# Perceiver block tail on one Trainium2 core: v projected ahead of k, q turned between the two products with Wo, token shift as two scaled matrix products

## Chip, cores and metric

One core of a Trainium2 chip. The metric is the device time in microseconds (us) of one execution of the whole program; lower is better.

## The reference, cut to what matters

The input is x (128 tokens, 256 channels) and a context of 12,544 rows of 256 channels. The block has three residual parts, each on a layer norm of x.

```python
x = x + xattn(layernorm(x), ctx)      # similarity over 12,544 context rows, softmax, mixing, W_qv
x = x + attn(layernorm(x))            # 16 heads, no softmax:
    # q, k, v = x@Wq+bq, x@Wk+bk, x@Wv+bv;  q, k = rope(q), rope(k)
    # score = q k^T / sqrt(16);  ctx = score v;  ctx @ Wo + bo
x = x + ffn(layernorm(x))
    # x_prev = concat([zeros, x[:, :-1]], axis=1)
    # xr = mu_r * x + (1 - mu_r) * x_prev;  xk = mu_k * x + (1 - mu_k) * x_prev
    # sigmoid(xr @ W_r) * (relu(xk @ W_k)**2 @ W_v)
```

As there is no softmax in the second part, the kernel computes k^T v first (16x16 blocks on the diagonal of a 256x256 matrix, kept by a mask) and multiplies it with Wo and then with q.

## The kernel before, in words

All order is written out by hand: each engine has one instruction stream (`block.sync`, `gpsimd`, `scalar`, `vector`, `tensor`), and the streams meet in semaphores alone. Nothing overtakes on an engine, so an instruction that waits holds all behind it.

**The sweep, 0 to 93 us.** The context comes in 25 chunks of 512 rows (the last has 256), first as keys (transposed), then as rows, through a ring of ten buffers in SBUF; SP issues all these loads. For most key chunks ScalarE makes a high part in a reduced 32-bit format (L476), VectorE subtracts it to get the low part (L681), and TensorE makes the scores in three products (L908, L912, L915); every fourth chunk is taken in plain fp32 (L898). VectorE keeps the running maximum (L703). In the second half, for each rows chunk k:

- TensorE turns the probabilities of chunk k+2 in four passes (L929), then runs `mix(k)` (L958, L960), which needs the low part of the rows and the low part of the turned probabilities.
- ScalarE exponentiates (L495), copies the turned probabilities as their high part (L508), and casts the first half of rows chunk k+2 (L476).
- POOL casts the second half of rows chunk k (L429, loop L425). This needs a free buffer pair, so `mix(k-4)` must be done. Between casts POOL has small jobs on weights and biases, at k = 15 to 19: among them `mean_const` (L445) and `mu_left`, that is 1 - mu for r and k (L447), at k = 17, and at k = 18 `w_neg_mean` (L452) and the sum of two weight blocks of 128x512 (L456), which the tail needs.
- VectorE, in this order: low part of the turned probabilities of k (`probs_low`, L710), then low part of rows chunk k+2 (`rows_low`, L681), which needs both casts of that chunk.

**The tail, 93 to 113 us.** TensorE: x1 is summed (L977), then `project` (L1051) for k, v and q, with the variance of x1 (L1061) between the first and the second half of the first projection; v^T times the rotated bias of k (L1074) and v^T times rotated k (L1078); `open_sums` (L972) and the part of x1 that is kept (L1082); masked product times Wo (L1086), in two halves; q turned (L1089), in two halves; product with q (L1094); means (L1103); two idle passes; the transposed and normed x2 (L1110), made by a product with a diagonal matrix; two more idle passes (`keep_warm`, L883, whose results nobody reads); k's projection (L1116), r's (L1122) and the last product (L1128). VectorE: variance, then for k `rope` (L819, L822), v scaled (L835), `rope_sum` (L828), `rope` for q, the mask (L841), `rope_sum` for q, bias of q added to the turned q (L847), statistics of x2 (L673 to L677), diagonal matrix (L853), shift (L859), square of relu (L864), gate (L870), sum (L875). POOL raises the variance to the power -1/2 (L421). ScalarE copies the two Wo results (L645) and x2 (L648), scales the transposed x2 by mu for k (L651) and for r (L659), relu (L665), sigmoid (L667).

In the shift before, the transposed x2 is in PSUM. ScalarE writes mu * x for all tokens, then VectorE adds (1 - mu) times the columns 0 to 126 to the columns 1 to 127: once for each half and each of k and r.

An fp32 product appears as two records on TensorE, a transpose as one.

Of the kernel before, what the change touches and what calls it, by code (L numbers as in the profile page):

```python
# [7 lines left out]
P = 128  # L8
# [3 lines left out]
ALU = mybir.AluOpType  # L12
ACT = mybir.ActivationFunctionType
# [4 lines left out]
DH = D // P  # L18
# [22 lines left out]
WB_Q = 4 * DH  # L41
WB_K = WB_Q + DH
WB_V = WB_K + DH
# [7 lines left out]
VC_W1, VC_W2, VC_W3, VC_MUR, VC_MUK, VC_BQ, VC_BQ_SWAPPED = (DH * n for n in range(7))  # L51
# [6 lines left out]
def build(nc, x, keys_in, keys_last_in, rows_in, rows_last_in, weights_in, vec_in, bias_in, const_in, out):  # L58
# [37 lines left out]
    with ExitStack() as stack:  # L96
        def sb(name, shape, dt=F32):
            return stack.enter_context(nc.sbuf_tensor(name, shape, dt))
# [4 lines left out]
        def sem(name):  # L103
            return stack.enter_context(nc.semaphore(name))
# [9 lines left out]
        ident = sb("ident", [P, P])  # L114
        ones = sb("ones", [P, P])
        idle = sb("idle", [P, CHUNK], BF16)
        w = sb("w", [P, WB, D])
        vec = sb("vec", [P, VC])
# [22 lines left out]
        ln_rstd = sb("ln_rstd", [P, 3])  # L141
# [27 lines left out]
        mean_const = sb("mean_const", [P, 1])  # L169
        mu_left = sb("mu_left", [P, 2 * DH])  # L170
        d_inv = sb("d_inv", [P, 1])
# [12 lines left out]
        with_cos, with_sin, rotated = scratch[:, 5:7, :], scratch[:, 7:9, :], scratch[:, 9:11, :]  # L184
        v = scratch[:, 11, :]
# [6 lines left out]
        rstd_diagonal = sb("rstd_diagonal", [P, P])  # L192

        xk_t = sb("xk_t", [P, DH, P])
        xr_t = sb("xr_t", [P, DH, P])
# [9 lines left out]
        banks = [scores_ps[:, g, h * CHUNK:(h + 1) * CHUNK] for g in range(3) for h in range(2)]  # L205
# [19 lines left out]
        tail_idle_ps = banks[2]  # L225
        x2n_ps = (banks[0][:, 0:P], banks[5][:, 0:P])
        k_t_ps = (banks[1][:, 0:P], banks[2][:, 0:P])
# [61 lines left out]
        mean_const_done = sem("mean_const_done")  # L289
        mu_left_done = sem("mu_left_done")  # L290
        x_c_done = sem("x_c_done")
# [47 lines left out]
        x2_done = sem("x2_done")  # L339
        diagonal_done = sem("diagonal_done")  # L340
        x2n_turned = sem("x2n_turned")

        xk_scaled = sem("xk_scaled")
        xr_scaled = sem("xr_scaled")
        xk_done = sem("xk_done")
# [64 lines left out]
        def _(pool):  # L410
# [8 lines left out]
            def power(n):  # L419
                pool.wait_ge(var_done, n + 1)  # L420
                nc.gpsimd.tensor_tensor(out=ln_rstd[:, n:n + 1], in0=ln_var[:, n:n + 1], in1=minus_half[:, :],  # L421
                                        op=ALU.pow).then_inc(rstd_done, 1)

            power(0)
            for k in range(EARLY, FULL):  # L425
                item, use = CHUNKS + k, row_use(k)
# [16 lines left out]
                if k == 17:  # L443
                    pool.wait_ge(b_mean_summed, 1)
                    nc.gpsimd.tensor_tensor(out=mean_const[:, :], in0=b_mean_sum[:, :], in1=ln_mv[:, 0, 0:1], op=ALU.add)\  # L445
                        .then_inc(mean_const_done, 1)
                    nc.gpsimd.tensor_scalar(mu_left[:, :], vec[:, VC_MUR:VC_MUR + 2 * DH], -1.0, 1.0,  # L447
                                            ALU.mult, ALU.add).then_inc(mu_left_done, 1)
                if k == 18:
# [16 lines left out]
        def _(act):  # L466
# [182 lines left out]
            for a in range(DH):  # L649
                act.wait_ge(x2n_turned, a + 1)  # L650
                nc.scalar.activation(xk_t[:, a, :], x2n_ps[a], ACT.Copy, scale=vec[:, VC_MUK + a:VC_MUK + a + 1])\  # L651
                    .then_inc(xk_scaled, 1)
            act.wait_ge(mean_const_done, 1)
            act.wait_ge(x2_mean_summed, 1)
            nc.scalar.activation(x2_mean[:, :], x2_mean_ps, ACT.Identity, bias=mean_const[:, :], scale=-1.0)\
                .then_inc(x2_mean_done, 1)
            for a in range(DH):
                act.wait_ge(xk_done, a + 1)
                nc.scalar.activation(xr_t[:, a, :], x2n_ps[a], ACT.Copy, scale=vec[:, VC_MUR + a:VC_MUR + a + 1])\  # L659
                    .then_inc(xr_scaled, 1)  # L660
            act.wait_ge(x2_mean_done, 1)
# [8 lines left out]
        def _(dve):  # L670
# [159 lines left out]

            dve.wait_ge(rstd_done, 2)
            dve.wait_ge(k_rows_projected, 1)
            rope(0, k_ps)
            dve.wait_ge(v_projected, 1)
            nc.vector.scalar_tensor_tensor(v, v_ps, ln_rstd[:, 1:2], bv_rows, ALU.mult, ALU.add).then_inc(v_done, 1)  # L835
            rope_sum(0)
# [8 lines left out]
            for a in range(DH):  # L845
# [6 lines left out]
            dve.wait_ge(rstd_done, 3)  # L852
            nc.vector.tensor_scalar(rstd_diagonal[:, :], ident[:, :], ln_rstd[:, 2:3], None, ALU.mult)\  # L853
                .then_inc(diagonal_done, 1)
            dve.wait_ge(mu_left_done, 1)
            for mixed_t, left, scaled, done in ((xk_t, DH, xk_scaled, xk_done), (xr_t, 0, xr_scaled, xr_done)):
                for a in range(DH):
                    dve.wait_ge(scaled, a + 1)
                    nc.vector.scalar_tensor_tensor(mixed_t[:, a, 1:P], x2n_ps[a][:, 0:P - 1],  # L859
                                                   mu_left[:, left + a:left + a + 1], mixed_t[:, a, 1:P],  # L860
                                                   ALU.mult, ALU.add).then_inc(done, 1)
# [17 lines left out]
        def _(pe):  # L879
# [208 lines left out]
            for a in range(DH):  # L1088
# [18 lines left out]
            pe.wait_ge(x2_c_done, 1)  # L1107
            pe.wait_ge(diagonal_done, 1)
# [80 lines left out]
```

## Time and profile before

| | us |
|---|---|
| median of 3 runs | 114.57 |
| lowest, highest | 114.46, 115.26 |
| the profiled execution | 115.56 |
| its span, first to last instruction | 113.8 |
| TensorE busy in it | 106.9 |
| VectorE busy | 92.9 |
| ScalarE busy | 80.4 |
| POOL busy | 29.0 |

The granted TensorE clock was 1.00 over the whole span, the higher of its two levels (2.4 GHz). Lines of the timeline give start, duration, engine, line of the kernel, operation, destination and sources, shapes, count, and in brackets the idle time before with what ended it. VectorE, ScalarE and TensorE start an instruction somewhat before the record of the last one ends, so records overlap.

### The profile page before, as it was taken

How to read it: one execution, taken by the hardware profiler on the slowest of the kernel's cores; microseconds unless marked ns; L12 is line 12 of the kernel's file. 1: busy time of each engine (PE TensorE's matmuls, PEld its weight loads, DVE VectorE, ACT ScalarE, POOL GpSimd, SP SyncE). 2: the span in 40 equal slices, each digit the busy share in tenths (PEclk: the TensorE clock that was granted, in tenths of full speed). 3: DMA queues.
4: the chain of work that ended last, by engine and by line, in shares of the span. 5: the costliest groups of instructions: out<-in, count | busy, mean ns of one | idle time of the engine just before them, and what ended most of it. 6: DMA issues, size and time to landing. Idle time of an engine off the chain costs nothing.

```text
span 113.8 us, 1825 instructions
## 1 busy us (share of the span) xinstructions
PE 106.9 (94%) x578; PEld 85.0 (75%) x579; DVE 92.9 (82%) x149; ACT 80.4 (71%) x168; POOL 29.0 (25%) x42
## 2 busy tenths in 40 slices
PE   5978999999999999999999999999899999898890
PEld 2426858585758588889999898999787899787680
DVE  1538999998999999988997999895999955693342
ACT  5039493889999874999999998999968444303450
POOL 2100000000000016204767567799621000100100
PEclk9999999999999999999999999999999999999999
DMA  3999999999999999999999999940000000000001
GB/s 94 353 370 418 415 419 422 419 422 416 419 425 418 419 408 415 422 354 383 351 396 414 416 423 421 419 169 0 6 0 0 0 6 0 0 0 0 6 3 46
DMA packets 8220, 29.82 MB, mean 262 GB/s; under 512 B 1042, under 2 KB 1298, under 8 KB 8082
## 3 DMA queue, kind: packets, MB, share of 16 engines
q1 hardware_dynamic: 8064, 29.69, 65.5%
q8 instruction: 5, 0.08, 0.3%
q14 instruction: 5, 0.04, 0.1%
q10 hardware_dynamic: 146, 0.01, 0.1%
HBM read 29.57 MB, written 0.13 MB: 261 GB/s over the span
## 4 chain that ended last, share of the span: by engine, by line
PE 85%; DMA 5%; DVE 3%; ACT 2%; issue 1%; SPq 1%; POOL 1%; DVEq 0%; ACTq 0%; POOLq 0%
PE mixed_ps L958 17%; PE scores_ps L929 9%; PE mixed_ps L960 8%; PE scores_ps L898 8%; PE scores_ps L908 8%; PE scores_ps L915 8%; PE scores_ps L912 7%; DMA raw<-keys_dram 5%; PE scores_ps L940 3%; PE scores_ps L1051 2%; PE mixed_ps L1103 1%; PE side_ps L977 1%; PE scores_ps L1116 1%; PE side_ps L1094 1%; PE scores_ps L977 1%
## 5 line engine op out<-in xcount | busy, mean ns | idle before, releaser
L681 DVE TENSOR_TENSOR pair<-raw,pair 128x1024 fp32r<-128x1024 f32 (+1 forms) x41 | 50.1, 1234 | 5.0 <-ACT pair L476 3.7
L476 ACT ACTIVATE pair<-raw 128x512 fp32r<-128x512 f32 (+1 forms) x41 | 33.4, 814 | 9.1 <-DMA raw<-keys_dram 5.7
L429 POOL CAST pair<-raw 128x512 fp32r<-128x512 f32 x22 | 21.3, 969 | 54.8 <-DMA raw<-rows_dram 39.3
L958 PE MATMUL mixed_ps<-pair,turned_high 128*128 128x512 f32 x84 | 32.2, 417 | 0.5 <-DVE turned_low L710 0.4
L960 PE MATMUL mixed_ps<-pair,turned_low 128*128 128x256 f32 x84 | 23.6, 281 | 0.0
L958 PEld LDWEIGHTS mixed_ps<-pair,turned_high 128*128 128x128 f32 x84 | 15.8, 188 | 4.2 <-issue 1.3
L703 DVE TENSOR_SCALAR_CACHE_REDUCE neg_scores<-scores_ps,neg_max 128x1024 f32<-128x1024 f32 (+2 forms) x14 | 16.1, 1147 | 0.4
L960 PEld LDWEIGHTS mixed_ps<-pair,turned_low 128*128 128x128 f32 x84 | 15.9, 190 | 0.0
L710 DVE TENSOR_TENSOR turned_low<-scores_ps,turned_high 128x512 fp32r<-128x512 f32 (+1 forms) x23 | 15.4, 671 | 0.3 <-ACT turned_high L508 0.3
L929 PE MATMUL scores_ps<-ident,neg_scores 128*128 128x128 f32 x98 | 14.6, 272 | 0.0
L908 PE MATMUL scores_ps<-pair,q_high 128*128 128x512 f32 x36 | 13.4, 453 | 1.1 <-ACT pair L476 1.1
L508 ACT ACTIVATE turned_high<-scores_ps 128x512 fp32r<-128x512 f32 (+1 forms) x23 | 13.2, 574 | 1.2 <-PE scores_ps L929 1.2
L495 ACT ACTIVATE neg_scores<-neg_scores,neg_max 128x1024 f32<-128x1024 f32 (+2 forms) x14 | 13.6, 974 | 0.1
L929 PEld LDWEIGHTS scores_ps<-ident,neg_scores 128*128 128x128 f32 x98 | 11.7, 140 | 1.6 <-ACT neg_scores L495 0.3
L898 PE MATMUL scores_ps<-raw,q_t 128*128 128x512 f32 (+1 forms) x28 | 12.4, 564 | 0.0
L915 PE MATMUL scores_ps<-pair,q_high 128*128 128x512 f32 x36 | 11.3, 396 | 0.0
L912 PE MATMUL scores_ps<-pair,q_low 128*128 128x512 f32 x36 | 11.2, 392 | 0.0
L908 PEld LDWEIGHTS scores_ps<-pair,q_high 128*128 128x128 f32 x36 | 6.6, 188 | 5.3 <-issue 4.3
L915 PEld LDWEIGHTS scores_ps<-pair,q_high 128*128 128x128 f32 x36 | 6.6, 188 | 2.0 <-DVE pair L681 0.6
L912 PEld LDWEIGHTS scores_ps<-pair,q_low 128*128 128x128 f32 x36 | 6.8, 188 | 1.5
L898 PEld LDWEIGHTS scores_ps<-raw,q_t 128*128 128x128 f32 x28 | 5.1, 189 | 3.4 <-issue 2.9
L421 POOL TENSOR_TENSOR ln_rstd<-ln_var,minus_half 128x1 f32<-128x1 f32 x3 | 1.7, 557 | 21.6 <-DVE ln_var L815 12.6
(187 smaller groups left out, 121.8 us busy)
## 6 DMA issues: line engine op xcount, KB each, us to landing
raw<-keys_dram SPq DMA_DIRECT2D x24, 512.0 KB, 10.1
raw<-rows_dram SPq DMA_DIRECT2D x24, 512.0 KB, 7.8
w<-weights_dram SPq DMA_DIRECT2D x1, 1792.0 KB, 9.6
w<-weights_dram SPq DMA_DIRECT2D x2, 512.0 KB, 11.6
const<-const_dram SPq DMA_DIRECT2D x1, 832.0 KB, 11.2
raw<-keys_last_dram SPq DMA_DIRECT2D x1, 256.0 KB, 8.4
raw<-rows_last_dram SPq DMA_DIRECT2D x1, 256.0 KB, 6.5
x_sb<-x_dram SPq DMA_DIRECT2D x1, 128.0 KB, 2.2
```

What stands on the lines that cost most here:

```text
L429: nc.gpsimd.tensor_copy(out=pair[:, use % PAIR_BUFS, 0, 2 * D:4 * D], in_=raw[:, slot(item), 2 * D:4 * D])\
L476: nc.scalar.activation(pair[:, use % PAIR_BUFS, 0, 0:columns], raw[:, slot(item), 0:columns], ACT.Copy)\
L681: nc.vector.tensor_tensor(out=pair[:, use % PAIR_BUFS, 1, 0:columns], in0=raw[:, slot(item), 0:columns], in1=pair[:, use % PAIR_BUFS, 0, 0 ...
L703: nc.vector.tensor_scalar(neg_scores[:, first_col:last_col], scores_ps[:, first // 2 % 3, scores_at:scores_at + last_col - first_col], -1. ...
L710: nc.vector.tensor_tensor(out=turned_low[:, k % TURNED_BUFS, 0:width_of(k)], in0=probs_turned_ps[k % TURNED_BUFS][:, 0:width_of(k)], in1=t ...
L898: last = nc.tensor.matmul(out_ps, q_t[:, a, :], keys_part(raw[:, slot(k), :], k, a), start=(a == 0), stop=(a == DH - 1))
L908: nc.tensor.matmul(out_ps, q_high[:, a, :], keys_part(high, k, a), start=(a == 0), stop=False)
L912: nc.tensor.matmul(out_ps, q_low[:, a, :], keys_part(high, k, a), start=False, stop=False)
L915: last = nc.tensor.matmul(out_ps, q_high[:, a, :], keys_part(low, k, a), start=False, stop=(a == DH - 1))
L929: last = nc.tensor.transpose(probs_turned_ps[k % TURNED_BUFS][:, t * P:(t + 1) * P], neg_scores[:, col:col + P], ident[:, :])
L958: nc.tensor.matmul(mixed_ps[:, :].rearrange("p (h d) -> p h d", h=2), probs_high, both[:, :, t * D:(t + 1) * D], start=(k == EARLY and t = ...
L960: last = nc.tensor.matmul(mixed_ps[:, 0:D], probs_low, rows_tile(high, t), start=False, stop=(k == LATE - 1 and end))
```

## The change

Constants: two 128x128 matrices are made on POOL right after the first power. `next_token` has ones on the diagonal beside the main one (it moves each token to the next), `same_less_next` is the identity less `next_token`. `mu_left` goes.

```diff
             power(0)
+            nc.gpsimd.memset(next_token[:, :], 0.0).then_inc(next_zeroed, 1)
+            pool.wait_ge(next_zeroed, 1)
+            nc.gpsimd.affine_select(out=next_token[:, :], in_=next_token[:, :], compare_op=ALU.not_equal, fill=1.0,
+                                    base=1, pattern=[[-1, P]], channel_multiplier=1).then_inc(shifts_set, 1)
+            pool.wait_ge(shifts_set, 1)
+            nc.gpsimd.tensor_tensor(out=same_less_next[:, :], in0=ident[:, :], in1=next_token[:, :], op=ALU.subtract)\
+                .then_inc(shifts_set, 1)
...
-                    nc.gpsimd.tensor_scalar(mu_left[:, :], vec[:, VC_MUR:VC_MUR + 2 * DH], -1.0, 1.0,
-                                            ALU.mult, ALU.add).then_inc(mu_left_done, 1)
```

v ahead of k, on VectorE and on TensorE:

```diff
             dve.wait_ge(rstd_done, 2)
+            dve.wait_ge(v_projected, 1)
+            nc.vector.scalar_tensor_tensor(v, v_ps, ln_rstd[:, 1:2], bv_rows, ALU.mult, ALU.add).then_inc(v_done, 1)
             dve.wait_ge(k_rows_projected, 1)
             rope(0, k_ps)
-            dve.wait_ge(v_projected, 1)
-            nc.vector.scalar_tensor_tensor(v, v_ps, ln_rstd[:, 1:2], bv_rows, ALU.mult, ALU.add).then_inc(v_done, 1)
             rope_sum(0)
...
-            project(k_ps, WB_K, 0)
+            project(v_ps, WB_V, 0)
...
-            project(k_ps, WB_K, 1).then_inc(k_rows_projected, 1)
-            for out_ps, block_row, done in ((v_ps, WB_V, v_projected), (q_ps, WB_Q, q_projected)):
+            project(v_ps, WB_V, 1).then_inc(v_projected, 1)
+            for out_ps, block_row, done in ((k_ps, WB_K, k_rows_projected), (q_ps, WB_Q, q_projected)):
```

q turned between the two halves of the product with Wo:

```diff
                 nc.tensor.matmul(attn_ps[a], vk[:, a, :], wo_c[:, a, :], start=True, stop=True).then_inc(attn_summed, 1)
-            pe.wait_ge(rotated_done, 2)
-            for a in range(DH):
-                nc.tensor.transpose(q_turn_ps[a], rotated[:, 1, a * P:(a + 1) * P], ident[:, :])\
-                    .then_inc(q_rot_turned, 1)
+                if a == 0:
+                    pe.wait_ge(rotated_done, 2)
+                    for b in range(DH):
+                        nc.tensor.transpose(q_turn_ps[b], rotated[:, 1, b * P:(b + 1) * P], ident[:, :])\
+                            .then_inc(q_rot_turned, 1)
```

The shift: TensorE makes the previous token (`prev_ps`) and the step from it to the token itself (`step_ps`) with the two constants scaled by the reciprocal deviation; ScalarE copies the first, VectorE makes mu * step + prev for all 128 tokens in place of 127.

```diff
+                act.wait_ge(prev_turned, a + 1)
+                nc.scalar.activation(prev_t[:, a, :], prev_ps[a], ACT.Copy).then_inc(prev_copied, 1)
-                nc.scalar.activation(xk_t[:, a, :], x2n_ps[a], ACT.Copy, scale=vec[:, VC_MUK + a:VC_MUK + a + 1])\
-                    .then_inc(xk_scaled, 1)
...
-                nc.scalar.activation(xr_t[:, a, :], x2n_ps[a], ACT.Copy, scale=vec[:, VC_MUR + a:VC_MUR + a + 1])\
-                    .then_inc(xr_scaled, 1)
...
-            nc.vector.tensor_scalar(rstd_diagonal[:, :], ident[:, :], ln_rstd[:, 2:3], None, ALU.mult)\
-                .then_inc(diagonal_done, 1)
+            nc.vector.tensor_scalar(to_next[:, :], next_token[:, :], ln_rstd[:, 2:3], None, ALU.mult)\
+                .then_inc(to_next_done, 1)
+            nc.vector.tensor_scalar(to_step[:, :], same_less_next[:, :], ln_rstd[:, 2:3], None, ALU.mult)\
+                .then_inc(to_step_done, 1)
...
-                    nc.vector.scalar_tensor_tensor(mixed_t[:, a, 1:P], x2n_ps[a][:, 0:P - 1],
-                                                   mu_left[:, left + a:left + a + 1], mixed_t[:, a, 1:P],
+                    dve.wait_ge(prev_copied, a + 1)
+                    dve.wait_ge(x2n_turned, a + 1)
+                    nc.vector.scalar_tensor_tensor(mixed_t[:, a, :], step_ps[a], vec[:, col + a:col + a + 1], prev_t[:, a, :],
                                                    ALU.mult, ALU.add).then_inc(done, 1)
...
-                nc.tensor.matmul(x2n_ps[a], x2_c[:, a * P:(a + 1) * P], rstd_diagonal[:, :], start=True, stop=True)\
+                nc.tensor.matmul(prev_ps[a], x2_c[:, a * P:(a + 1) * P], to_next[:, :], start=True, stop=True)\
+                    .then_inc(prev_turned, 1)
+            pe.wait_ge(to_step_done, 1)
+            for a in range(DH):
+                nc.tensor.matmul(step_ps[a], x2_c[:, a * P:(a + 1) * P], to_step[:, :], start=True, stop=True)\
                     .then_inc(x2n_turned, 1)
             keep_warm(WARM_SHIFT, tail_idle_ps)
```

## Rows read from the trace of the kernel before

**Rows 1.** The page, part 4: shares of the chain that ended last, by engine.

```profile
PE 85%; DMA 5%; DVE 3%; ACT 2%; issue 1%; SPq 1%; POOL 1%; DVEq 0%; ACTq 0%; POOLq 0%
```

**Rows 2.** The chain in order of time, 78 to 82 us: start, duration, what.

```profile
78.69 0.62 POOL pair L429
...
79.33 0.92 DVE pair L681
...
80.47 0.70 DVE turned_low L710
...
81.30 0.47 PE mixed_ps L958
```

**Rows 3.** Timeline of the second half of the sweep, 73 to 84 us.

```profile
74.47 1.22 DVE L681 TENSOR_TENSOR pair<-raw,pair 128x1024 fp32r<-128x1024 f32 x1
74.54 1.20 POOL L447 TENSOR_SCALAR mu_left<-vec 128x4 f32<-128x4 f32 x1
...
75.63 0.62 ACT L476 ACTIVATE pair<-raw 128x512 fp32r<-128x512 f32 x1
...
75.68 0.61 POOL L429 CAST pair<-raw 128x512 fp32r<-128x512 f32 x1
...
76.36 1.23 DVE L681 TENSOR_TENSOR pair<-raw,pair 128x1024 fp32r<-128x1024 f32 x1
76.41 2.33 POOL L456 TENSOR_TENSOR w<-w 128x512 f32<-128x512 f32 x1
...
76.97 0.48 PE L958 MATMUL mixed_ps<-pair,turned_high 128*128 128x512 f32 x1
...
78.82 0.48 PE L958 MATMUL mixed_ps<-pair,turned_high 128*128 128x512 f32 x1
...
79.39 1.63 POOL L429 CAST pair<-raw 128x512 fp32r<-128x512 f32 x1
...
83.07 0.61 POOL L429 CAST pair<-raw 128x512 fp32r<-128x512 f32 x1 [1.49 <-PE mixed_ps L960]
83.18 1.58 DVE L681 TENSOR_TENSOR pair<-raw,pair 128x1024 fp32r<-128x1024 f32 x1
```

**Rows 4.** Timeline of the attention part of the tail, 97 to 105 us.

```profile
97.95 1.54 PE L1051 MATMUL scores_ps<-w,x_t 128*128 128x256 f32 x6
98.96 0.48 DVE L819 SCALAR_TENSOR_TENSOR neg_scores<-scores_ps,ln_rstd,const 128x256 f32<-128x256 f32 x1 [0.68 <-POOL ln_rstd L421]
...
100.15 0.42 DVE L828 TENSOR_TENSOR neg_scores<-neg_scores 128x256 f32<-128x256 f32 x1
...
101.71 0.41 DVE L828 TENSOR_TENSOR neg_scores<-neg_scores 128x256 f32<-128x256 f32 x1
...
101.86 1.03 PE L1086 MATMUL scores_ps<-wo_c,neg_scores 128*128 128x257 f32 x4
102.49 0.82 ACT L645 ACTIVATE attn<-scores_ps 128x257 f32<-128x257 f32 x2 [4.79 <-PE scores_ps L1086]
...
102.73 0.38 PE L1089 MATMUL scores_ps<-ident,neg_scores 128*128 128x128 f32 x2
...
103.45 1.13 PE L1094 MATMUL side_ps<-attn,neg_scores 128*128 128x256 f32 x4 [0.34 <-DVE neg_scores L847]
```

**Rows 5.** Timeline of the token shift, 106 to 109 us.

```profile
106.56 0.68 PE L1110 MATMUL scores_ps<-rstd_diagonal,x_c 128*128 128x128 f32 x4
...
107.05 0.63 ACT L651 ACTIVATE xk_t<-scores_ps,vec 128x128 f32<-128x128 f32 x2 [1.58 <-PE scores_ps L1110]
107.08 0.59 PE L883 MATMUL scores_ps<-idle 128*128 128x512 bf16 x2
107.52 0.61 DVE L859 SCALAR_TENSOR_TENSOR xk_t<-scores_ps,mu_left,xk_t 128x127 f32<-128x127 f32 x2 [1.11 <-ACT xk_t L651]
...
107.92 1.16 PE L1116 MATMUL scores_ps<-xk_t,w 128*128 128x128 f32 x8 [0.25 <-DVE xk_t L859]
```

**Rows 6.** Waits of TensorE in the whole span: who for whom, us, times, longest.

```profile
PE scores_ps L908 <- ACT pair L476: 1.1, 1, 1.1
```

More of the change, by code:

```diff
@@ L114, in build @@
         ident = sb("ident", [P, P])
+        next_token = sb("next_token", [P, P])
+        same_less_next = sb("same_less_next", [P, P])
         ones = sb("ones", [P, P])
@@ L169, in build @@
         mean_const = sb("mean_const", [P, 1])
-        mu_left = sb("mu_left", [P, 2 * DH])
         d_inv = sb("d_inv", [P, 1])
@@ L191, in build @@
         x2 = sb("x2", [P, D])
-        rstd_diagonal = sb("rstd_diagonal", [P, P])
+        to_next = sb("to_next", [P, P])
+        to_step = sb("to_step", [P, P])
+        prev_t = sb("prev_t", [P, DH, P])
         xk_t = sb("xk_t", [P, DH, P])
@@ L225, in build @@
         tail_idle_ps = banks[2]
-        x2n_ps = (banks[0][:, 0:P], banks[5][:, 0:P])
+        prev_ps = (banks[0][:, 0:P], banks[5][:, 0:P])
+        step_ps = (banks[3][:, 0:P], banks[4][:, 0:P])
         k_t_ps = (banks[1][:, 0:P], banks[2][:, 0:P])
@@ L289, in build @@
         mean_const_done = sem("mean_const_done")
-        mu_left_done = sem("mu_left_done")
         x_c_done = sem("x_c_done")
@@ L339, in build @@
         x2_done = sem("x2_done")
-        diagonal_done = sem("diagonal_done")
+        next_zeroed = sem("next_zeroed")
+        shifts_set = sem("shifts_set")
+        prev_turned = sem("prev_turned")
+        prev_copied = sem("prev_copied")
+        to_next_done = sem("to_next_done")
+        to_step_done = sem("to_step_done")
         x2n_turned = sem("x2n_turned")
-        xk_scaled = sem("xk_scaled")
-        xr_scaled = sem("xr_scaled")
         xk_done = sem("xk_done")
@@ L649, in _ @@
             for a in range(DH):
-                act.wait_ge(x2n_turned, a + 1)
-                nc.scalar.activation(xk_t[:, a, :], x2n_ps[a], ACT.Copy, scale=vec[:, VC_MUK + a:VC_MUK + a + 1])\
-                    .then_inc(xk_scaled, 1)
+                act.wait_ge(prev_turned, a + 1)
+                nc.scalar.activation(prev_t[:, a, :], prev_ps[a], ACT.Copy).then_inc(prev_copied, 1)
             act.wait_ge(mean_const_done, 1)
@@ L656, in _ @@
                 .then_inc(x2_mean_done, 1)
-            for a in range(DH):
-                act.wait_ge(xk_done, a + 1)
-                nc.scalar.activation(xr_t[:, a, :], x2n_ps[a], ACT.Copy, scale=vec[:, VC_MUR + a:VC_MUR + a + 1])\
-                    .then_inc(xr_scaled, 1)
             act.wait_ge(x2_mean_done, 1)
@@ L852, in _ @@
             dve.wait_ge(rstd_done, 3)
-            nc.vector.tensor_scalar(rstd_diagonal[:, :], ident[:, :], ln_rstd[:, 2:3], None, ALU.mult)\
-                .then_inc(diagonal_done, 1)
-            dve.wait_ge(mu_left_done, 1)
-            for mixed_t, left, scaled, done in ((xk_t, DH, xk_scaled, xk_done), (xr_t, 0, xr_scaled, xr_done)):
+            dve.wait_ge(shifts_set, 2)
+            nc.vector.tensor_scalar(to_next[:, :], next_token[:, :], ln_rstd[:, 2:3], None, ALU.mult)\
+                .then_inc(to_next_done, 1)
+            nc.vector.tensor_scalar(to_step[:, :], same_less_next[:, :], ln_rstd[:, 2:3], None, ALU.mult)\
+                .then_inc(to_step_done, 1)
+            for mixed_t, col, done in ((xk_t, VC_MUK, xk_done), (xr_t, VC_MUR, xr_done)):
                 for a in range(DH):
-                    dve.wait_ge(scaled, a + 1)
-                    nc.vector.scalar_tensor_tensor(mixed_t[:, a, 1:P], x2n_ps[a][:, 0:P - 1],
-                                                   mu_left[:, left + a:left + a + 1], mixed_t[:, a, 1:P],
+                    dve.wait_ge(prev_copied, a + 1)
+                    dve.wait_ge(x2n_turned, a + 1)
+                    nc.vector.scalar_tensor_tensor(mixed_t[:, a, :], step_ps[a], vec[:, col + a:col + a + 1], prev_t[:, a, :],
                                                    ALU.mult, ALU.add).then_inc(done, 1)
@@ L1086, in _ @@
                 nc.tensor.matmul(attn_ps[a], vk[:, a, :], wo_c[:, a, :], start=True, stop=True).then_inc(attn_summed, 1)
-            pe.wait_ge(rotated_done, 2)
-            for a in range(DH):
-                nc.tensor.transpose(q_turn_ps[a], rotated[:, 1, a * P:(a + 1) * P], ident[:, :])\
-                    .then_inc(q_rot_turned, 1)
+                if a == 0:
[3 more added lines that the diff above has]
+                            .then_inc(q_rot_turned, 1)
             for a in range(DH):
@@ L1107, in _ @@
             pe.wait_ge(x2_c_done, 1)
-            pe.wait_ge(diagonal_done, 1)
+            pe.wait_ge(to_next_done, 1)
             for a in range(DH):
-                nc.tensor.matmul(x2n_ps[a], x2_c[:, a * P:(a + 1) * P], rstd_diagonal[:, :], start=True, stop=True)\
+                nc.tensor.matmul(prev_ps[a], x2_c[:, a * P:(a + 1) * P], to_next[:, :], start=True, stop=True)\
[3 more added lines that the diff above has]
+                nc.tensor.matmul(step_ps[a], x2_c[:, a * P:(a + 1) * P], to_step[:, :], start=True, stop=True)\
                     .then_inc(x2n_turned, 1)
```

## The prediction, made before the change was run

> **What bounds the kernel now.** I read first the shares of the chain that ended last, then that chain in order of time, then the timeline of each stretch that the diff touches. The shares say that TensorE is on the path for 85% of the span [rows 1]: work on another engine pays only where TensorE waits for it. The chain in order leaves TensorE in two places that the edits reach. The first is the middle of the key sweep: at 78.69 the path goes to POOL's cast of rows chunk 19, from there to VectorE's subtraction for the same chunk at 79.33, to its subtraction for the turned probabilities at 80.47, and back to TensorE at 81.30 [rows 2]. The second is the tail from 97 us on, a string of short steps, where I followed which operand of each product comes last. The profiled execution took 115.56 us with a span of 113.8; the median shown is 114.57. I work with differences in the span and put them on the median.
>
> **Part 1, v ahead of k.** The same projections run in the same slots, only the contents change places. The six passes from 97.95 end at 99.49, the end of the second matrix, now k's [rows 4]. VectorE starts at 98.96, when the reciprocal deviation is there, and its three products before the sum at 100.15 are spaced (100.15 - 98.96)/3 = 0.40. Now v's comes at 98.96 and k's could start at 99.36, but k lands at 99.49 and is seen some 0.04 later: 99.53, a loss of 0.17. The sum of the rotation now stands right behind the second product it reads, with nothing between: 99.53 + 0.40 + 0.48 (that product's own time) + 0.04 = 100.45 against 100.15, 0.30 late, and done at 100.87. Behind it in VectorE's queue stand q's two rotations, the two masks, and q's sum: that one moves from 101.71 to 102.01 and ends at 102.42.
> On TensorE v is ready earlier, so the first two v products start without their wait; before, that wait was at most some 0.2 us. The products with k's rotation then wait for 100.87 + 0.05, and the first pass after a wait costs 0.10 more (four passes of 0.215 with a last one of 0.38 would make 1.03, the row at 103.45 has 1.13). So they begin in effect at 101.02. Before they began 1.0 us (four passes of 0.11, the opening 0.11, four passes of 0.11) ahead of the product with Wo at 101.86, at 100.86. So the first product with Wo moves from 101.86 to 102.02: this part costs 0.16.
>
> **Part 2, q turned between the two products with Wo.** Before: four passes of (102.73 - 101.86)/4 = 0.22, two turns of 0.11, then VectorE adds the bias and the product with q starts at 103.45; its second half is long fed. ScalarE's copies of the two Wo results take 0.82 together, 0.39 each. After: Wo's first half 102.02 to 102.46, then the turns, for which q's sum must be there: 102.42 + 0.05 = 102.47, on the edge, and with the refill of 0.10 they start at 102.57; second half of Wo 102.79 to its result at 103.39; copy 103.42 to 103.81. TensorE sees a ScalarE result later than one of VectorE (I take 0.12; 0.05 and 0.2 are the ends), so the last two passes start at 103.96 in place of 103.88 (103.45 + 2 x 0.215). The end of x2's sum is 0.06 late by this (104.64 for 104.58). With part 2 alone the same sum gives 0.2 early, with every handover of part 1 at 0.1 more it gives 0.35 late. So parts 1 and 2 cancel: +0.06, ends -0.25 and +0.35. What is late next is no longer q's turn but ScalarE's second copy.
>
> **Part 3, the token shift.** VectorE scales two 128x128 matrices, not one: the first is on the path as before, the second is done 0.2 to 0.3 us later, while TensorE runs the first four passes. Before: products from 106.56, ScalarE's scaling from 107.05, VectorE's sum from 107.52, k's projection from 107.92 [rows 5]. After: four passes for the previous token, four more for the step (0.44), results at about 107.52 + 0.06 (the step) and 107.49 (ScalarE's copy, 0.3, and its handover). The sum starts at 107.56 and k's projection could at 107.95. But the two idle passes meant to keep the clock up, 0.22 each [rows 5], now stand behind eight passes, not four, and end at 106.56 + 0.06 + 0.07 + 0.88 + 0.43 = 108.00. The projection starts there, without a refill, where it started in effect at 107.92 + 0.10. Gain 0.02; ends -0.1 and +0.15. That r's input comes 0.3 us sooner and that ScalarE loses two operations is worth nothing: TensorE runs k's, r's and the last projection back to back from 107.92 on. Three small POOL operations at the start run before any rows come; beside them q is made, and TensorE later waits 1.1 us for ScalarE's first split of keys anyway [rows 6], so they are hidden up to 1.1 us.
>
> **Part 4, what leaves POOL.** With the shift on TensorE the four-column operation mu_left (1.20 us at 74.54) is gone from POOL's queue. This is the largest effect I find, through who gets the SBUF port. The rows show exclusion. When VectorE's subtraction with two SBUF inputs starts first, POOL stands: started 0.05 or 0.06 later, a cast of 0.61 takes 1.63, the sum of two weight blocks (w, 128x512) 2.33, the tiny mu_left 1.20. When a cast starts first, by 0.11 (83.07 against 83.18), VectorE's 1.23 becomes 1.58, ending 1.08 after the cast [rows 3]. The Trainium skill, SBUF — State Buffer, "Who interferes with whom", says the same of such pairs: whichever issues first has the shared port for its whole instruction. By that rule POOL's head start below decides, and the time would be the forecast's.
> Now chunk 18. Its cast needs product 14, which began two cadences of 78.82 - 76.97 = 1.85 before product 16 (76.97), so was over by 75.1. It then stands behind VectorE's subtraction of 74.47 and ends 1.69 after that start (79.33 to 79.39 + 1.63 likewise): 76.16 for 76.29. The weight sum, 0.12 behind, starts at 76.28 and not 76.41. VectorE's subtraction at 76.36 is held by ScalarE's cast (75.63 + 0.62 = 76.25, plus 0.11), so stays. The order turns: POOL is first by 0.08.
> The weight sum then takes its own 2.33 - 1.08 + 0.05 = 1.30 and ends at 77.58; VectorE's subtraction ends 1.08 later, 78.65 for 77.59; product 17 starts at 79.39 for 78.82, 0.57 late. But the cast of 19, at 78.69 before, no longer queues behind a blocked weight sum. If VectorE gets the port at the seam, that cast ends at 79.11, the subtraction of 19 starts at 79.17, product 18 at 81.25, and from there VectorE starts each subtraction before POOL's cast of the chunk. Before it lost that race three times (81.07, 83.18, 85.28; one row stands), with 1.50 + 0.60 = 2.10 per chunk against TensorE's cadence of 1.85. Products 19, 20 and 21 then keep 1.85: 0.8 us gained. If POOL's next cast takes the port once more, product 17 slips to 79.97, and the same steps leave 0.25. The rows at 75.68 to 76.41 show VectorE slipping in between two POOL operations, which leans to 0.8; no row has it already waiting there. I take 0.5.
>
> **Sum.** +0.06 - 0.02 - 0.5 = about -0.5: 114.57 - 0.5 = 114.1 us.
>
> **The rivals.** A, the forecast, 114.1 us, 45%; its own range is 113.7 to 114.4.
> B, no change: 0.08 us is less than the smallest lead with which POOL wins in the rows (0.11), and VectorE wins at -0.05, so the weight sum may still come second. Then it ends where it did, 76.36 + 2.38 = 78.74, cast 19 follows at 78.69, and only the tail is left: 114.57 + 0.04 = 114.6 us, 30%. For it: the lead hangs on a ScalarE cast. Against it: 0.08 lies nearer to 0.11 than to -0.05.
> C, slower: k's rotation behind v. The 0.30 goes down VectorE's queue to q's sum, and the turns that need it now stand before Wo's second half. It decides once that sum is later than 102.46, when TensorE has done Wo's first half; by my sum it is at 102.47. From there each 0.1 us goes through Wo, the copy and the last product. With B and the upper end of +0.35: 114.9 us, 12%. For it: no slack at all. Against it: it wants each handover above its row.
> D, both gains whole: the port at 0.8 and the tail at its lower end of -0.25: 113.5 us, 13%. Against it: k's delay of 0.17 follows from the order of the passes alone.
>
> **How the numbers follow.** A, B and D and most of C lie between 113.4 and 114.9, the range. About 1%, 1.15 us, is what a measurement of this kernel can tell from no change. Only the far side of D passes it downwards: 0.09. Upwards it wants C and something unseen beside: 0.03. Within 1%: 0.88.
>
> **What would show it.** Part 1: k's first product on VectorE near 99.5, its sum near 100.45 (relative to the variance), q's sum after 102. Part 2: the last product's second half released by ScalarE's second copy. Part 3: idle passes ending at the start of k's projection; r never waiting. Part 4: POOL's weight sum 1.3 us long and VectorE's subtraction beside it 2.3, and no subtraction of 1.58 afterwards. Wrong would be: a weight sum still 2.33 long with a large gain, k's rotation not late, or x2's sum earlier by more than 0.25.

## The result, and the profile after the change

The change takes 114.03 us (median of 20 runs, 113.5 to 115.38) against 114.94 us before (20 runs, 114.34 to 116.41): ratio 0.9914, 95% interval 0.9887 to 0.9941. The ratio leaves out the few executions that were over 1.5% slower than the fastest of the same kernel; it stands for 0.99 us (0.68 to 1.30), where the medians of all runs differ by 0.91. The forecast was a gain of 0.5 us, from 114.57 to 114.1, with a range that holds 114.03. The time came out as forecast, the gain twice as large: the kernel before, 114.57 in the 3 runs that the forecast started from, takes 114.94 in 20. The profiled execution of the change took 113.73 us with a span of 111.9.

First the chain of the page, part 4, of the changed kernel: shares by engine.

```profile
PE 64%; DMA 17%; DVE 10%; issue 3%; ACT 2%; POOL 1%; SPq 1%; DVEq 0%; ACTq 0%; POOLq 0%
```

Against [rows 1] this looks like another kernel, but most of it is the start of the span: in this execution the chain happens to lead back to the loading of keys. The two spans differ by 1.9 us, and half of that is there before the sweep reaches the place that the diff touches: VectorE's subtraction for chunk 17, which stood at 74.47 in [rows 3], stands at 73.53 here. Over all profiles of this study that moment lies between 73.2 and 74.7 us with no relation to the edits (73.34 and 74.65 in two kernels that keep the start of before, e12 and e11 below), so I count from it. From there to the variance of x1 it was 98.12 - 74.47 = 23.65 us and is 96.18 - 73.53 = 22.65: the 1.00 us of the change. Here is the place (product k is `mix(k)`, the products of TensorE for rows chunk k), in the timeline of the changed kernel (L687 is the old L681, L716 the old L710, L442 the cast, L467 the sum of the two weight blocks):

```profile
73.53 1.22 DVE L687 TENSOR_TENSOR pair<-raw,pair 128x1024 fp32r<-128x1024 f32 x1
74.12 1.10 POOL L442 CAST pair<-raw 128x512 fp32r<-128x512 f32 x1 [0.48 <-PE mixed_ps L968]
...
75.33 1.28 POOL L467 TENSOR_TENSOR w<-w 128x512 f32<-128x512 f32 x1
75.42 2.28 DVE L687 TENSOR_TENSOR pair<-raw,pair 128x1024 fp32r<-128x1024 f32 x1
76.57 1.60 POOL L442 CAST pair<-raw 128x512 fp32r<-128x512 f32 x1
77.62 0.68 DVE L716 TENSOR_TENSOR turned_low<-scores_ps,turned_high 128x512 fp32r<-128x512 f32 x1
...
78.22 1.21 DVE L687 TENSOR_TENSOR pair<-raw,pair 128x1024 fp32r<-128x1024 f32 x1
78.27 1.64 POOL L442 CAST pair<-raw 128x512 fp32r<-128x512 f32 x1
78.45 0.47 PE L966 MATMUL mixed_ps<-pair,turned_high 128*128 128x512 f32 x1 [0.32 <-DVE turned_low L716]
```

Read it against [rows 3]. There the weight sum began 0.05 us behind the subtraction and took 2.33 us; here it begins 0.09 us ahead and takes 1.28, and the subtraction takes 2.28. Product 17 (78.45) is late by half a microsecond, 2.42 us after product 16 (76.03) where the cadence is 1.85, and no later subtraction is stretched. Products 18 to 21 follow at the cadence, and 22 in 1.63 us:

```profile
76.03 0.48 PE L966 MATMUL mixed_ps<-pair,turned_high 128*128 128x512 f32 x1
...
80.29 0.48 PE L966 MATMUL mixed_ps<-pair,turned_high 128*128 128x512 f32 x1
...
82.14 0.48 PE L966 MATMUL mixed_ps<-pair,turned_high 128*128 128x512 f32 x1
...
87.48 0.48 PE L966 MATMUL mixed_ps<-pair,turned_high 128*128 128x512 f32 x1
```

Product 22 begins 11.45 us after product 16, before it was 12.39. The tail, in the timeline of the changed kernel, gives nothing and takes a little:

```profile
96.18 0.16 DVE L821 TENSOR_SCALAR ln_var<-scores_ps 128x1 f32<-128x1 f32 x1 [0.19 <-PE scores_ps L1069]
97.02 0.48 DVE L839 SCALAR_TENSOR_TENSOR neg_scores<-scores_ps,ln_rstd,const 128x256 f32<-128x256 f32 x1 [0.68 <-POOL ln_rstd L427]
97.58 0.48 DVE L825 SCALAR_TENSOR_TENSOR neg_scores<-scores_ps,ln_rstd,const 128x256 f32<-128x256 f32 x1
...
98.56 0.43 DVE L834 TENSOR_TENSOR neg_scores<-neg_scores 128x256 f32<-128x256 f32 x1
99.05 0.71 PE L1086 MATMUL scores_ps<-neg_scores 128*128 128x128 f32 x4 [0.19 <-DVE neg_scores L834]
...
100.56 0.22 PEld L1098 LDWEIGHTS scores_ps<-ident,neg_scores 128*128 128x128 f32 x2 [0.17 <-DVE neg_scores L834]
100.63 0.38 PE L1098 MATMUL scores_ps<-ident,neg_scores 128*128 128x128 f32 x2
...
101.48 0.39 ACT L656 ACTIVATE attn<-scores_ps 128x257 f32<-128x257 f32 x1 [0.27 <-PE scores_ps L1094]
102.72 0.43 DVE L679 BATCH_NORM_STATS2 ln_six<-side_ps 128x6 f32<-128x256 f32 x1 [1.22 <-PE side_ps L1103]
...
105.67 0.82 DVE L868 SCALAR_TENSOR_TENSOR xk_t<-scores_ps,vec,prev_t 128x128 f32<-128x128 f32 x2 [0.96 <-ACT prev_t L662]
...
106.07 0.99 PEld L1129 LDWEIGHTS scores_ps<-xk_t,w 128*128 128x128 f32 x8 [0.35 <-DVE xk_t L868]
...
109.30 0.48 DVE L883 TENSOR_TENSOR x<-mixed_out,x 128x128 f32<-128x128 f32 x2
```

From the variance of x1 to the statistics of x2 it is 102.72 - 96.18 = 6.54 us (before 6.50), from there to the last sums 109.30 - 102.72 = 6.58 (before 6.51). k's rotation starts where its projection lands (97.58), its sum comes 2.38 us after the variance (before 2.03), and ScalarE's second copy (101.48) is what the last product waits for. PEld is TensorE's loading of weights: for the turns of q (100.56) and for k's projection (106.07) it sat idle until VectorE's result was there. The three stretches add up to 1.00 - 0.04 - 0.07 = 0.89 us.

### The profile page after: what moved, and what is told of

The parts are those of the page before. It is cut to its first block, busy times and chain, and to the rows that moved or that the text cites. A ratio compares the mean times of both kernels' runs of the same rounds, so it can differ in the third digit from the quotient of the medians.

```text
span 111.9 us, 1840 instructions
## 1 busy us (share of the span) xinstructions
PE 106.8 (95%) x583; PEld 85.3 (76%) x583; DVE 93.5 (84%) x150; ACT 79.6 (71%) x166; POOL 31.8 (28%) x44
## 4 chain that ended last, share of the span: by engine, by line
PE 64%; DMA 17%; DVE 10%; issue 3%; ACT 2%; POOL 1%; SPq 1%; DVEq 0%; ACTq 0%; POOLq 0%
DMA raw<-keys_dram 17%; PE mixed_ps L966 15%; PE scores_ps L937 8%; PE mixed_ps L968 8%; DVE pair L687 6%; PE scores_ps L906 4%; PE scores_ps L923 4%; PE scores_ps L948 3%; PE scores_ps L920 3%; PE scores_ps L916 3%; ACT pair L487 2%; PE scores_ps L1059 2%; PE mixed_ps L1112 1%; PE side_ps L985 1%; DVE turned_low L716 1%
## 5 line engine op out<-in xcount | busy, mean ns | idle before, releaser
L687 DVE TENSOR_TENSOR pair<-raw,pair 128x1024 fp32r<-128x1024 f32 (+1 forms) x41 | 50.4, 1243 | 2.5 <-ACT pair L487 2.4
L442 POOL CAST pair<-raw 128x512 fp32r<-128x512 f32 x22 | 25.3, 1151 | 51.0 <-DMA raw<-rows_dram 38.4
L716 DVE TENSOR_TENSOR turned_low<-scores_ps,turned_high 128x512 fp32r<-128x512 f32 (+1 forms) x23 | 15.4, 671 | 0.4 <-ACT turned_high L519 0.3
```

Source lines behind the costliest of these rows:

```text
L442: nc.gpsimd.tensor_copy(out=pair[:, use % PAIR_BUFS, 0, 2 * D:4 * D], in_=raw[:, slot(item), 2 * D:4 * D])\
L687: nc.vector.tensor_tensor(out=pair[:, use % PAIR_BUFS, 1, 0:columns], in0=raw[:, slot(item), 0:columns], in1=pair[:, use % PAIR_BUFS, 0, 0 ...
L716: nc.vector.tensor_tensor(out=turned_low[:, k % TURNED_BUFS, 0:width_of(k)], in0=probs_turned_ps[k % TURNED_BUFS][:, 0:width_of(k)], in1=t ...
```

## The experiments

The theory: the change gains because mu_left leaves POOL's queue. That moves the weight sum from just behind to just ahead of VectorE's subtraction, so it gets first the way into SBUF that the two engines share (the port); afterwards VectorE wins each race against a cast and TensorE keeps its cadence. The rivals: the gain is in the tail, or POOL's queue was only too long. Each run is read in three stretches: A from the subtraction of chunk 17 to the variance of x1, B from there to the statistics of x2, C from there to the last sums.

**e1, mu_left early.** On the kernel before:

```diff
             power(0)
+            pool.wait_ge(vec_loaded, 16)
+            nc.gpsimd.tensor_scalar(mu_left[:, :], vec[:, VC_MUR:VC_MUR + 2 * DH], -1.0, 1.0,
+                                    ALU.mult, ALU.add).then_inc(mu_left_done, 1)
...
-                    nc.gpsimd.tensor_scalar(mu_left[:, :], vec[:, VC_MUR:VC_MUR + 2 * DH], -1.0, 1.0,
-                                            ALU.mult, ALU.add).then_inc(mu_left_done, 1)
```

> The kernel before, with one move: POOL makes mu_left right after its first power, at about 5 us, and no longer between the casts at 74.5 us. The tail stays as before. Port theory: the sum of the two weight blocks starts just ahead of VectorE's subtraction, is 1.3 us long and not 2.33, the subtraction beside it 2.3, no later subtraction is 1.58 long, and the whole gain of the change is here: ratio to before 0.991 to 0.992 (0.9 to 1.0 us). Rival, the tail's edits bring the gain: ratio 1.000.

Measured: 114.31 us against 114.82, ratio 0.9942 (0.9912 to 0.9972). The timeline of e1 has the pattern of the change:

```profile
75.23 1.29 POOL L457 TENSOR_TENSOR w<-w 128x512 f32<-128x512 f32 x1
75.32 2.28 DVE L682 TENSOR_TENSOR pair<-raw,pair 128x1024 fp32r<-128x1024 f32 x1
```

A is 22.62 us, 1.03 less than before, with the tail of before. The sweep's gain is thus all in this one move. The ratio missed the expected 0.991 to 0.992, and the profile shows a part of the reason: C took 7.58 us in place of 6.51. The windows of e1 show the cause (the column before the last two is the granted clock):

```profile
103.00:104.00 1.00, 1.00 (x11) 1.00 (x11) 0.34 (x2) 0.38 (x1) 0.54 (x1) 1.00 0.00 0
104.00:105.00 1.00, 0.92 (x5) 0.70 (x6) 0.29 (x1) 0.00 (x0) 0.01 (x1) 0.69 0.00 0
105.00:106.00 1.00, 1.00 (x6) 0.55 (x4) 0.25 (x1) 0.66 (x3) 0.00 (x0) 0.50 0.07 16
106.00:107.00 1.00, 1.00 (x6) 0.85 (x5) 0.91 (x4) 1.00 (x5) 0.00 (x0) 0.50 0.03 8
107.00:108.00 1.00, 1.00 (x7) 1.00 (x7) 0.24 (x1) 0.42 (x2) 0.00 (x0) 0.60 0.00 0
```

TensorE's clock went from 2.4 to 1.2 GHz for some 3 us. Four of the 12 runs of e1 have a mean clock of 0.985 like this one, and 2 of the 31 runs of before beside it. Without these runs the medians are 114.09 and 114.81, a difference of 0.72 us, still short of the 1.03 of stretch A; the rest is not explained. That was a second question: does the change also keep the clock up, and by which part?

**e2, mu_left kept.** The changed kernel with the operation put back at k = 17, its result unused.

```diff
                     nc.gpsimd.tensor_tensor(out=mean_const[:, :], in0=b_mean_sum[:, :], in1=ln_mv[:, 0, 0:1], op=ALU.add)\
                         .then_inc(mean_const_done, 1)
+                    nc.gpsimd.tensor_scalar(mu_left[:, :], vec[:, VC_MUR:VC_MUR + 2 * DH], -1.0, 1.0,
+                                            ALU.mult, ALU.add).then_inc(mu_left_done, 1)
```

> The changed kernel, with the four-column mu_left kept in its old place in POOL's queue (nobody reads it). Port theory: the weight sum starts behind VectorE's subtraction again and takes 2.33 us, three subtractions take 1.58, and the gain is gone: ratio to before 1.000 to 1.001. Rival, the tail brings the gain: ratio 0.991 as for the change.

Measured: 114.87 us, ratio 1.0008 (0.9979 to 1.0037). A is 23.65 as before. The whole tail of the change is in this kernel, and it shows no gain in the median.

**e3, the weight sum 0.15 us later.**

```diff
                     pool.wait_ge(w3_scaled, DH)
+                    nc.gpsimd.tensor_tensor(out=spare[:, :], in0=b_mean[:, 0:1], in1=b_mean[:, 1:2], op=ALU.add)
                     nc.gpsimd.tensor_tensor(out=w[:, 0:DH, :], in0=w[:, 0:DH, :], in1=w[:, 3 * DH:4 * DH, :],
```

> The changed kernel with one one-column addition (0.15 us from start to start, result unused) put right ahead of the weight sum in POOL's queue. Port theory: POOL's lead of 0.09 us turns into a lag of 0.06, so VectorE gets the port, the weight sum takes 2.3 us, and some 0.9 us are lost for 0.15 us of work: ratio to before 1.000. Rival, POOL's queue was only too long by 1.2 us: 0.15 us at most are lost, ratio 0.991 to 0.993.

Measured: 115.05 us, ratio 0.9995 (0.9963 to 1.0028). The timeline of e3:

```profile
76.27 0.19 POOL L468 TENSOR_TENSOR spare<-b_mean 128x1 f32<-128x1 f32 x1
76.36 1.23 DVE L689 TENSOR_TENSOR pair<-raw,pair 128x1024 fp32r<-128x1024 f32 x1
76.42 2.32 POOL L469 TENSOR_TENSOR w<-w 128x512 f32<-128x512 f32 x1
...
81.07 1.58 DVE L689 TENSOR_TENSOR pair<-raw,pair 128x1024 fp32r<-128x1024 f32 x1
...
83.18 1.59 DVE L689 TENSOR_TENSOR pair<-raw,pair 128x1024 fp32r<-128x1024 f32 x1
```

The lead of 0.09 us has become a lag of 0.06, and A is 23.66: one column of work on POOL, 0.15 us, costs 1.0 us. That rules out the length of the queue and leaves the order of two starts.

**e4, k ahead of v again**, q still turned between the products with Wo.

```diff
-            project(v_ps, WB_V, 0)
+            project(k_ps, WB_K, 0)
...
-            for out_ps, block_row, done in ((k_ps, WB_K, k_rows_projected), (q_ps, WB_Q, q_projected)):
+            for out_ps, block_row, done in ((v_ps, WB_V, v_projected), (q_ps, WB_Q, q_projected)):
```

VectorE's order goes back with it: k's rotation, then v.

> The changed kernel with k projected and rotated ahead of v again, q still turned between the two products with Wo. By my sum v first costs 0.16 us on the way to the product with Wo and takes away the 0.2 us that the earlier turn would give: x2's sum ends 0.2 to 0.3 us sooner, measured from the variance of x1, ratio to before 0.989 (the change 0.991). Rival, v first is neutral or a gain: x2's sum ends no sooner.

Measured: 113.87 us, ratio 0.9892 (0.9857 to 0.9928); B is 102.72 - 96.46 = 6.26 us, 0.28 less than in the change. Here v first is a loss.

**e5, the weight sum last.**

```diff
-                if k == 18:
-                    pool.wait_ge(w3_scaled, DH)
-                    nc.gpsimd.tensor_tensor(out=w[:, 0:DH, :], in0=w[:, 0:DH, :], in1=w[:, 3 * DH:4 * DH, :],
-                                            op=ALU.add).then_inc(w_combined, 1)
...
+            pool.wait_ge(w3_scaled, DH)
+            pool.wait_ge(total_inv_done, 1)
+            nc.gpsimd.tensor_tensor(out=w[:, 0:DH, :], in0=w[:, 0:DH, :], in1=w[:, 3 * DH:4 * DH, :],
+                                    op=ALU.add).then_inc(w_combined, 1)
             power(1)
```

> The changed kernel with the sum of the two weight blocks moved behind POOL's last cast, where it also waits for VectorE's reciprocal of the total, so that it runs beside instructions with one SBUF input. Port theory: the sum is 1.3 us long, no VectorE subtraction is longer than 1.25 us, product 17 is no longer 0.5 us late, and that time is gained on top of the change: ratio to before 0.986 to 0.987. Rival, what matters is only the three stretched subtractions that the change already removed: ratio 0.991 as for the change.

Measured: 113.16 us, ratio 0.9846 (0.9806 to 0.9886); A is 95.52 - 73.43 = 22.09, another 0.56 us less, which is product 17's delay. The timeline of e5, POOL alone from 86 us on:

```profile
87.30 1.29 POOL L471 TENSOR_TENSOR w<-w 128x512 f32<-128x512 f32 x1 [2.88 <-DVE total_inv L772]
```

The windows of TensorE, VectorE and the rest from 75 to 90 us, of e5 (the first number after the stretch's length is TensorE busy):

```profile
75.00:90.00 15.00, 15.00 (x102) 13.63 (x101) 13.71 (x20) 12.85 (x27) 7.64 (x9) 1.00 0.01 2
```

and of the kernel before:

```profile
75.00:90.00 15.00, 14.54 (x89) 12.29 (x88) 13.82 (x17) 12.12 (x28) 7.80 (x10) 1.00 0.02 8
```

TensorE has no gap left there, and POOL is busy for about as long. The counts of products, 102 and 89, are not of the same work: at 90 us e5 is some 2.5 us further on than before. Nor is the gap of 0.46 us the whole loss of before, since the records run on into the waits: before, four turns start at 82.77 and last 0.60 us in the record, and the product behind them starts 0.63 us after them, where at 78.47 it follows in 0.35. The loss is read from A.

**e6, e4 and e5 together.**

> e5 with k projected and rotated ahead of v as in e4. If the two gains lie in different stretches they add: 0.5 us in the sweep and 0.28 us between the variance of x1 and the statistics of x2, ratio to before 0.983 to 0.985. Rival, one of them hides the other: ratio 0.986 to 0.988.

Measured: 113.14 us, ratio 0.9833 (0.9796 to 0.987). A is 22.09 and B 6.25: both gains stand side by side. The intervals of e5 and e6 overlap, so that e6 is the faster of the two rests on B alone. Both beat the kernel before, and by A also the change.

**e7, the old shift** (with mu_left at the start) under the new order of v, k and q: the diff of the shift undone.

> The changed kernel with the token shift of before (mu_left made at the start, as in e1), v first and q turned between kept. Statistics of x2 to the last sum: 6.5 us as before, 0.07 less than in the change. The granted clock fell to half for 3 us of the shift stage in 4 of 12 runs of e1 and in 2 of 31 of before, and in none of the 52 runs with the new shift. Theory that the new shift prevents it: some runs here have a mean clock of 0.985 and are 1.1 us longer, ratio to before 0.991 to 0.995. Rival, that the new order of v, k and q prevents it: no such run, ratio 0.990 to 0.991.

Measured: 113.87 us, ratio 0.9899 (0.986 to 0.9939); C is 6.50, and none of 6 runs has the low clock. The new shift costs 0.08 us.

**e8, the shift alone**: the changed kernel with k first and q turned behind both products.

> The changed kernel with k ahead of v and q turned behind both products with Wo, so that the constants, the new shift and POOL's shorter queue are all that is left of the change. Variance of x1 to statistics of x2: 6.50 as before (6.54 in the change), then 6.58 as in the change: ratio to before 0.991. If the new shift prevents the fall of the clock, no run has 0.985; if the order of v, k and q does, about a third of the runs have it and the ratio is 0.993 or more.

Measured: 114.01 us, ratio 0.9913 (0.9873 to 0.9952); B is 6.50. One of 8 runs has the low clock, the profiled one, with C = 8.01 us. So the new shift does not prevent the fall. TensorE waits once in the attention part of this kernel, ahead of the product with q; its weight loads sit idle there for 0.6 us. In the change they sit idle twice, 0.31 and 0.33 us, ahead of either half of that product. Waits of TensorE in e8, 100 to 104 us:

```profile
PE side_ps L1102 <- DVE neg_scores L853: 0.3, 1, 0.3
```

**e9, no idle passes**: e6 without the call below.

```diff
-            keep_warm(WARM_SHIFT, tail_idle_ps)
```

> e6 without the two idle passes between the shift's products and k's projection. In the change the projection starts where these passes end, though its input is there some 0.1 us earlier. If they are only in the way: statistics of x2 to the last sum 6.48 to 6.52 us in place of 6.59, and the clock stays. If they are needed: the clock falls in some runs, which are 1.1 us or more longer.

Measured: 113.35 us, ratio 0.9846 (0.9797 to 0.9896); C is 6.58, not the expected 6.48 to 6.52. TensorE now waits for VectorE where the passes stood:

```profile
106.23 1.19 PE L1128 MATMUL scores_ps<-xk_t,w 128*128 128x128 f32 x8 [0.29 <-DVE xk_t L868]
```

So the idle passes did not set the start of k's projection; its input did. None of 6 runs has the low clock.

**e10, v first alone**: the changed kernel with q turned behind both products.

> The changed kernel with q turned behind both products with Wo again, v still first. By my sum v first alone costs 0.16 us: variance of x1 to statistics of x2 6.66 us (before 6.50, the change 6.54), ratio to before 0.991 to 0.993. Theory that the turn between the products keeps the clock up: some runs here have a mean clock of 0.985. Rival, v first does it: none.

Measured: 115.1 us, ratio 0.9982 (0.994 to 1.0023). B is 103.78 - 97.00 = 6.78, so v first alone costs 0.28 us, not 0.16. And 5 of 12 runs have a mean clock of 0.985. They are a part of why the ratio missed the expected 0.991 to 0.993: without such runs the medians are 114.79 here and 114.86 before. But A, B and C of the profile promise 1.04 - 0.28 - 0.08 = 0.68 us less than before; why these runs do not show it stays open.

**e11, the turn alone** on the kernel before.

```diff
+                if a == 0:
+                    pe.wait_ge(rotated_done, 2)
+                    for b in range(DH):
+                        nc.tensor.transpose(q_turn_ps[b], rotated[:, 1, b * P:(b + 1) * P], ident[:, :])\
+                            .then_inc(q_rot_turned, 1)
```

> The kernel before with q turned between the two products with Wo and nothing else. By my sum part 2 alone makes x2's sum 0.2 us earlier: variance of x1 to statistics of x2 6.26 to 6.30 us in place of 6.50; the sweep as before (weight sum 2.33 us long). If this turn is what keeps the clock up, no run has a mean clock of 0.985 (before: 8 of 61), ratio to before 0.996 to 0.998; if not, about one run in seven has it.

Measured: 114.59 us against 115.1, ratio 0.9973 (0.9937 to 1.0009), which alone does not tell it from no change; B is 104.54 - 98.29 = 6.25 us, and none of 12 runs has the low clock.

**e12, the weight sum last, alone** on the kernel before.

> The kernel before with only the weight sum moved behind POOL's last cast, mu_left kept in its place. Port theory: without a long POOL operation between the casts no VectorE subtraction is stretched, whether mu_left is there or not, and the sweep is as short as in e5: 1.4 to 1.5 us gained, ratio to before 0.986 to 0.988. Rival, mu_left itself costs: 0.990 or more.

Measured: 113.2 us, ratio 0.9849 (0.979 to 0.9908); A is 95.44 - 73.34 = 22.10, 1.55 us less than before, with mu_left in its old place and still held up. The timeline of e12:

```profile
73.34 1.22 DVE L681 TENSOR_TENSOR pair<-raw,pair 128x1024 fp32r<-128x1024 f32 x1
73.41 1.20 POOL L447 TENSOR_SCALAR mu_left<-vec 128x4 f32<-128x4 f32 x1
```

A is that of e5, which has no mu_left there, so mu_left costs nothing by itself. One of 6 runs has the low clock.

All profiles in the three stretches, each the difference of two starts (us), and the runs with a mean clock of 0.985:

| kernel | A | B | C | low clock |
|---|---|---|---|---|
| before | 23.65 | 6.50 | 6.51 | 10 of 78 |
| the change | 22.65 | 6.54 | 6.58 | 0 of 20 |
| e1 mu_left early | 22.62 | 6.50 | 7.58 (low clock) | 4 of 12 |
| e2 mu_left kept | 23.65 | 6.55 | 6.58 | 0 of 12 |
| e3 sum later | 23.66 | 6.54 | 6.59 | 0 of 12 |
| e4 k first | 22.63 | 6.26 | 6.59 | 0 of 8 |
| e5 sum last | 22.09 | 6.54 | 6.59 | 0 of 6 |
| e6 both | 22.09 | 6.25 | 6.59 | 0 of 6 |
| e7 old shift | 22.65 | 6.54 | 6.50 | 0 of 6 |
| e8 shift only | 22.64 | 6.50 | 8.01 (low clock) | 1 of 8 |
| e9 no idle passes | 22.09 | 6.26 | 6.58 | 0 of 6 |
| e10 v first | 22.61 | 6.78 | 6.59 | 5 of 12 |
| e11 turn only | 23.64 | 6.25 | 6.51 | 0 of 12 |
| e12 sum last only | 22.10 | 6.49 | 6.51 | 1 of 6 |

(The 78 runs of before are those beside the twelve experiments.)

## Why the prediction was right, point by point

- Part 4, the port, was right in place, mechanism and order. The subtraction after 74.47 was to be followed by the weight sum ahead by 0.08 us: it was 0.09. The sum was to take 1.30 us: 1.28. Product 17 was to be 2.42 us behind product 16: it is. At the seam VectorE got the port, the branch that I had priced at 0.8 us. The step that failed is the size: I took 0.5, between 0.8 and 0.25, for want of a row, and the stretch gave 1.00. Rival B's condition, the weight sum second, did not come true. Up to product 21 my steps hold (9.83 us after product 16 for 9.82 measured, a gain of 0.83); the rest comes behind it, where VectorE was late before for the following chunks too (0.94 at product 22, 1.00 at the variance), which I had not followed.
- That 114.03 us lies so near the forecast of 114.1 is luck. The forecast started from 114.57, 0.37 us below the 114.94 that the same kernel takes in 20 runs, and its gain was 0.4 to 0.5 us too small; the two errors cancel. The forecast gain of 0.5 lies outside the measured 0.68 to 1.30. The sweep gave what rival D had for it and more, the tail did not. And where I said that about 1% is the least that can be told from no change, the interval tells 0.86% from it.
- e3 shows the cause, e2 and e1 bound it from both sides. With a lag of 0.06 us in place of the lead, VectorE wins and the gain is gone: what e3 does to the kernel is exactly B. The Trainium skill's rule (SBUF — State Buffer, "Who interferes with whom": whoever issues first holds the shared pair for the whole instruction) agrees with both traces: with a lead of 0.09 us the sum ran in 1.28 us and the subtraction took 2.28, with a lag of 0.06 the subtraction ran in 1.23 and the sum took 2.32.
- Part 1 was right in its steps, short in its size. k's rotation came 1.40 us after the variance (forecast 1.41), its sum 2.38 (2.33), the product with it 2.87 (2.80). Alone it costs 0.28 us (e10 against before) where I had 0.16. In e10 the product with Wo starts 3.97 us after the variance, for 3.74 before, where the forecast had 3.90, and then takes 1.08 us for 1.03. Most of the 0.07 us over the forecast is there when k's sum starts.
- Part 2 was right: turns in effect 4.45 us after the variance (forecast 4.45), second copy 5.30 (5.30). Alone it gives 0.25 us (e11), forecast 0.2. Together 6.54 for a forecast of 6.56. Rival C stood at its edge, as I had it: the weight load of the turns sat idle for 0.17 us until q's sum was there, and the turns began no later than forecast. Stretch B lost 0.04 us, far from C's 0.35. In this part I made a slip: 103.81 + 0.12 is 103.93 and not 103.96, and the last passes would then be 0.05 late.
- Part 3 was wrong in its reason. I had k's projection held by the idle passes and gaining 0.02; it loses 0.07 to 0.08 (e7), and e9 shows that the passes hold nothing. The failed term is the handover to the first sum: placed 2.88 us after the statistics (107.56 less the shifted 104.68), it came at 2.95 (before 2.90), now behind two waits, one for ScalarE and one for TensorE. k's projection starts at 3.35 (before 3.30) and takes 1.19 us for 1.16; with that the loss is accounted for. The 108.00 of this part also holds already the 0.06 of parts 1 and 2 that the sum adds once more, a slip of 0.06 us.
- What I missed altogether is the clock. It lifts the medians of e1 and e10, and 10 of 78 runs of before have it. In the two profiles that show a fall it adds 1.1 and 1.4 us; in none of the 88 runs of kernels that turn q between the products, as part 2 does, was there one.

## What to carry to other kernels

In a loop paced by one engine, look at which of two operations on POOL and VectorE starts first, not at how busy either is. Here 0.15 us decided which one held the port, and the loser's delay put the loop into a slower rhythm for three chunks (2.10 us per chunk for 1.85). The length of the operation counts too: one of two columns that POOL started 0.09 us ahead of the subtraction (78.13 and 78.22 in the change) left that at 1.21 us. A long POOL operation with SBUF inputs is better placed behind such a loop, beside VectorE instructions that read PSUM: there the sum took 1.29 us, and moving this one operation (e12) gave 1.5%. By the intervals of the whole runs that is not told from the change's 0.9%, by stretch A it is: 1.55 us for 1.00. And of a change in several parts, time the stretches apart: here one part lost 0.28 us, another gave 0.25, a third lost 0.08, and the gain lay in a line that was removed in passing.

## What the runs showed of the hardware that was not expected

The granted clock falls to 1.2 GHz for about 3 us in part of the executions of the same kernel: from 104.4 to 107.8 us in the profile of e1, from 104.6 to 108.0 in that of e8. What TensorE did before: the product with q in 1.13 us after a wait of 0.34 us, then 16 passes with one column. In the kernels that turn q behind both products with Wo, 21 of 116 runs have a mean clock of 0.985; in those that turn it between them, where that wait is cut in two, none of 88. It holds in each group of runs made side by side: 6 of 43 and 0 of 32 beside e1 to e4, 3 of 21 and 0 of 18 beside e5 to e8, 9 of 29 and 0 of 6 beside e9 and e10, 3 of 23 and 0 of 12 beside e11 and e12. The plainest pair is e10 against the change, which differ in this turn alone: 5 of 12 runs and 0 of 20. e11 against before agrees but is weak by itself: at the rate of before, 12 runs without a fall would come about one time in five. No run shows why the turn matters: e10, with v first, has the falls more often than before, though the wait is the same 0.34 us, so the length of that wait is not all. The price is 7.58 - 6.51 = 1.07 us in e1 and 8.01 - 6.58 = 1.43 in e8; what makes it larger in e8 was not tested.

The second of the two VectorE sums for k in the new shift starts 0.48 us behind the first (two records in 0.82 us, for 0.60 with r's pair). What it waits for I have not found; TensorE's eight passes behind it end at most 0.03 us later by it.
